# Product-key stage: the products and sums of the expert numbers on GpSimd behind its splitting of probabilities, the signed numbers one tile later on VectorE

## The reference, cut to what matters

```python
q = (x @ Wq + bq).reshape(-1, 8, 128)                 # 8 heads, two halves of 64
s1 = einsum('bhc,hnc->bhn', q[..., :64], keys[:, 0])  # 64 scores for each half
s2 = einsum('bhc,hnc->bhn', q[..., 64:], keys[:, 1])
s1t, i1 = top_k(s1, 8);  s2t, i2 = top_k(s2, 8)
all_scores = s1t[..., :, None] + s2t[..., None, :]    # 64 pairs
all_idx = i1[..., :, None] * 64 + i2[..., None, :]
scores, best = top_k(all_scores, 8)                   # 8 of the 64 pairs
indices = take_along_axis(all_idx, best)              # the expert numbers
inner = einsum('bd,bhkd->bhk', x, w_down[indices])
vals = relu(inner) * softmax(scores)
out = einsum('bhk,bhkd->bd', vals, w_up[indices])
```

## Time and profile before

| what | before |
|---|---|
| median of 3 runs | 1126.18 us (1122.7 to 1128.15) |
| the profiled execution | 1123.27 us |
| its span | 1121.3 us |
| busy in the span: PE, DVE, ACT, POOL | 86%, 73%, 45%, 36% |
| granted TensorE clock, mean of the span | 0.941 |

### The profile page before, as it was taken

The page is one execution under the profiler, slowest core; times in us unless marked ns, Lnnn a source line. Parts: engine busy times, 40 slices in busy tenths (PEclk is TensorE's granted clock), DMA queues, the critical chain, the costliest instruction groups (busy, mean ns, idle before and its releaser), DMA issues.

```text
span 1121.3 us, 21964 instructions
## 1 busy us (share of the span) xinstructions
PE 960.1 (86%) x8152; PEld 687.9 (61%) x8152; DVE 819.2 (73%) x2594; ACT 500.5 (45%) x1042; POOL 399.8 (36%) x335
## 2 busy tenths in 40 slices
PE   3587887996988888889888877899999988889997
PEld 3454444453878777778787875545545545467775
DVE  5666767568999999999999953466665565362887
ACT  1124555563344434434334332566565654344332
POOL 4664652000444453343333340455444454300000
PEclk9588999997899999999999897899999998989999
DMA  4101300000000000000000012000000000000000
GB/s 108 31 1 30 141 1 1 1 1 1 2 2 1 1 2 1 1 1 2 1 2 2 2 39 75 1 1 1 1 1 1 1 1 1 1 1 1 10 9 19
DMA packets 6720, 14.12 MB, mean 13 GB/s; under 512 B 1885, under 2 KB 4766, under 8 KB 6046
## 3 DMA queue, kind: packets, MB, share of 16 engines
q1 hardware_dynamic: 5598, 10.70, 2.9%
q0 software_dynamic: 1024, 2.10, 0.7%
HBM read 11.74 MB, written 1.05 MB: 11 GB/s over the span
## 4 chain that ended last, share of the span: by engine, by line
PE 53%; DVE 28%; issue 7%; ACT 6%; POOL 4%; DVEq 1%; POOLq 0%; DMA 0%; SPq 0%; ACTq 0%
PE quad L1859 5%; PE bank L1854 5%; PE quad L1740 4%; PE bank L1713 4%; DVE i L1134 4%; DVE w_v L1217 4%; PE bank L1765 4%; PE bank L1516 4%; PE bank L1751 4%; PE quad L1702 3%; PE bank L1629 3%; PE bank L1607 3%; PE bank L1535 2%; DVE one_u L1223 2%; ACT a_e L841 2%
## 5 line engine op out<-in xcount | busy, mean ns | idle before, releaser
L565 POOL TENSOR_TENSOR vals<-relu_in,g_sb 128x512 f32<-128x512 f32 x80 | 125.5, 1608 | 157.4 <-DVE one_u L1223 130.0
L600 POOL TENSOR_TENSOR a_e<-a_e,a_rrec 128x1024 f32<-128x1024 f32 x64 | 121.2, 1893 | 149.3 <-DVE a_rrec L1318 149.3
L1629 PE MATMUL bank<-xnT,wd 128*128 128x128 f32 x1024 | 141.1, 295 | 33.9 <-ACT relu_in L717 33.8
L1629 PEld LDWEIGHTS bank<-xnT,wd 128*128 128x128 f32 x1024 | 130.2, 205 | 45.8 <-ACT relu_in L717 41.8
L1713 PE MATMUL bank<-wu,vals 128*128 128x128 f32 x1024 | 119.5, 278 | 4.8 <-issue 4.8
L1713 PEld LDWEIGHTS bank<-wu,vals 128*128 128x128 f32 x1024 | 118.2, 195 | 4.9 <-issue 4.9
L841 ACT ACTIVATE a_e<-quad,a_negmax 128x512 f32<-128x512 f32 x128 | 86.8, 683 | 38.2 <-DVE a_negmax L1311 34.4
L1516 PE MATMUL bank<-a_kT,a_qT 32*128 32x512 f32 x344 | 83.7, 451 | 21.6 <-DVE a_q_aug L1026 13.4
L671 ACT ACTIVATE a_eT<-quad 128x512 f32<-128x512 f32 x128 | 73.9, 599 | 57.6 <-PE quad L1520 57.1
L1311 DVE TENSOR_REDUCE a_negmax<-quad 128x2 f32<-128x1024 f32 x64 | 77.9, 1217 | 22.3 <-PE quad L1740 21.6
L717 ACT ACTIVATE relu_in<-bank 128x512 f32<-128x512 f32 x128 | 73.6, 593 | 40.9 <-PE bank L1629 40.4
(11 more groups left out here) (229 smaller groups left out, 1903.3 us busy)
## 6 DMA issues: line engine op xcount, KB each, us to landing
wd<-in_pk_down SPq DMA_DIRECT2D x1, 2048.0 KB, 7.8
wu<-in_pk_up SPq DMA_DIRECT2D x1, 2048.0 KB, 12.3
wu<-in_moe_w SPq DMA_DIRECT2D x2, 1024.0 KB, 5.8
out<-h SPq DMA_DIRECT2D x4, 256.0 KB, 2.3
wd<-in_num_rows SPq DMA_DIRECT2D x1, 512.0 KB
a_eT<-in_pk_wqT SPq DMA_DIRECT2D x1, 512.0 KB, 6.4
a_eT<-in_pk_keys SPq DMA_DIRECT2D x1, 512.0 KB, 7.9
wu<-in_event_table,idx_e POOLq DMA_INDIRECT x16, 2.5
```

The costliest lines, as they stand in the source:

```text
L565: nc.gpsimd.tensor_tensor(*weigh_args(t, c, k, g_sb[:, slot, :])).then_inc(vals_pool, 1)
L600: nc.gpsimd.tensor_tensor(e1[:, g % 4], e1[:, g % 4], rrec1[:, g % 4].unsqueeze(2).to_broadcast([P, 2, S]), ALU.mult).then_inc(a1.nr, 1)
L1629: last = mm(bank[g % 2][:, q * P:(q + 1) * P], wd[:, IG * g + q, :], xnT_tile(t), start=True, stop=True)
```

## The change

The two products and six sums of the expert numbers leave VectorE and become a function of GpSimd, `pick_numbers`, that runs ahead of `split_p` of the same tile. VectorE keeps the comparisons and the softmax inverse. The two instructions for the signed numbers become a function of their own, `signed_numbers`, which VectorE runs one pass later, behind `one_hots` of the next tile. ScalarE's wait before it overwrites the candidates is set to the new count of `ij`.

```diff
+            def pick_numbers(t):
+                steps = 6 * t
+                pool.wait_ge(i8e_rdy, t + 1)
+                for s in range(2):
+                    pool.wait_ge(picked, 2 * t + s + 1)
+                    nc.gpsimd.tensor_tensor(ext[:, s], ext[:, s], i8e[:, s].rearrange("p a h k -> p a (h k)"),
+                                            ALU.mult).then_inc(ext_step, 1)
+                for s in range(2):
+                    pool.wait_ge(ext_step, steps + 1 + s)
+                    nc.gpsimd.tensor_tensor(ext[:, s, 0:4], ext[:, s, 0:4], ext[:, s, 4:8], ALU.add).then_inc(ext_step, 1)
+                for s in range(2):
+                    pool.wait_ge(ext_step, steps + 3 + s)
+                    nc.gpsimd.tensor_tensor(ext[:, s, 0:2], ext[:, s, 0:2], ext[:, s, 2:4], ALU.add).then_inc(ext_step, 1)
+                if t:
+                    pool.wait_ge(uv_rdy, t)
+                for s in (1, 0):
+                    pool.wait_ge(ext_step, steps + 5 + s)
+                    nc.gpsimd.tensor_tensor(ij[:, s], ext[:, s, 0], ext[:, s, 1], ALU.add).then_inc(ij_rdy, 1)
...
+            pick_numbers(0)
             split_p(0)
+            pick_numbers(1)
             split_p(1)
             for t in range(NT):
                 weigh_second(t)
...
                 if t + 2 < NT:
+                    pick_numbers(t + 2)
                     split_p(t + 2)
...
                 dve.wait_ge(bab_rdy, t + 1)
+                if t:
+                    dve.wait_ge(ij_rdy, 2 * t)
                 for s in range(2):
                     V.tensor_tensor(ext[:, s], bab[:, s:s + 1].to_broadcast([P, TOP, HK]), iota8[:],
-                                    ALU.is_equal).then_inc(ext_step, 1)
+                                    ALU.is_equal).then_inc(picked, 1)
...
                 V.reciprocal(pz[:, 1], pz[:, 0]).then_inc(z_rec, 1)
-                dve.wait_ge(i8e_rdy, t + 1)
-                for s in range(2):
-                    dve.wait_ge(ext_step, steps + s + 1)
-                    V.tensor_tensor(ext[:, s], ext[:, s], i8e[:, s].rearrange("p a h k -> p a (h k)"),
-                                    ALU.mult).then_inc(ext_step, 1)
                 dve.wait_ge(z_rec, t + 1)
                 V.tensor_scalar(pz[:, 2], pz[:, 1], P_UNIT, None, ALU.mult).then_inc(z_rdy, 1)
...
-                for s in (1, 0):
-                    dve.wait_ge(ext_step, steps + 7 + s)
-                    V.tensor_tensor(ij[:, s], ext[:, s, 0], ext[:, s, 1], ALU.add).then_inc(ij_rdy, 1)
+
+            def signed_numbers(t):
+                both = [P, 2, HK]
                 if t:
                     dve.wait_ge(uvpT_ps, t)
                 dve.wait_ge(ij_rdy, 2 * t + 1)
...
             half_max(1)
+            signed_numbers(0)
             half_index(1, 0, 2 * H)
...
             one_v_half(0, 1)
+            signed_numbers(1)
 
             for t in range(NT):
                 one_hots(t)
+                if t and t + 1 < NT:
+                    signed_numbers(t + 1)
                 weigh(t, 1)
```

More of the change, by code:

```diff
@@ L375, in tower @@
         m8_rdy, pair_rdy, b8_rdy, bi_rdy, bab_rdy = sem("first_max"), sem("pair_scores"), sem("pair_max"), sem("pair_index"), sem("pair_position")
-        z_sum, z_rec, ext_step, one_v_rdy = sem("z_summed"), sem("z_reciprocal"), sem("one_of_eight_steps"), sem("one_v_ready")
+        z_sum, z_rec, ext_step, one_v_rdy = sem("z_summed"), sem("z_reciprocal"), sem("number_step"), sem("one_v_ready")
+        picked = sem("positions_compared")
         uvpT_ps, uvpT_sb, onehot = sem("uvpT_in_psum"), sem("uvpT_in_sbuf"), sem("onehot_ready")
@@ L723, in expand_indices @@
                 if t:
-                    act.wait_ge(ij_rdy, t)
+                    act.wait_ge(ij_rdy, 2 * t)
                 for s in range(2):
@@ L1166, in expert_numbers @@
             def expert_numbers(t):
-                both = [P, 2, HK]
-                steps = 8 * t
                 dve.wait_ge(bab_rdy, t + 1)
+                if t:
+                    dve.wait_ge(ij_rdy, 2 * t)
                 for s in range(2):
                     V.tensor_tensor(ext[:, s], bab[:, s:s + 1].to_broadcast([P, TOP, HK]), iota8[:],
-                                    ALU.is_equal).then_inc(ext_step, 1)
+                                    ALU.is_equal).then_inc(picked, 1)
                 if t:
```

## The result

The changed kernel is slower: 1140.28 us in the median (1138.86 to 1143.33), against 1124.44 for the kernel before on the same chip, some 16 us between the medians, and a ratio of 1.0152 with a 95% interval of 1.0113 to 1.0192 (brackets behind a ratio mean this interval throughout). The prediction had started from 1126.2, the median of the three runs known then. The profiled execution took 1141.13 us (1123.27 before), its span 1139.2.

The account below looks back on a forecast made before the run. VectorE was taken to set the 25.7 us pass. Adding 4.2, less 2.1 removed and 0.52 regained, gave +1.6 a pass, 22 over 14 passes; with 2.1 ahead of the loop, +24 took 1126.2 to 1150 us, range 1130 to 1177.

Parts of the forecast that it names:

- The added 4.2 us: Per pass, GpSimd's two products and six sums, 5.1 us alone, hold up VectorE's two-input instructions for 4.2 us.
- 2.1 removed: Per pass, VectorE loses products 0.63 us, sums 1.20 and L1201's hold-up 0.27, together 2.10 us.
- the first product's 0.79: GpSimd's first product: 1.06 us less 0.12 and less about 0.15 beside VectorE's softmax inverse and scaling.
- the check on `one_v`: Earlier `one_v` collision: VectorE's loss set against GpSimd's remaining time less 0.12, as 0.06 + 1.32 against 1.43 - 0.12.
- the cancelling rival: Per pass, a collision of about 2.6 us cancels 2.1 saved and 0.5 regained: 1121 to 1131 us, chance 8%.
- L1201's 0.27: Signed-number instruction L1201, meeting `split_p`'s last instruction, takes 0.55 us against its twin's 0.28; the 0.27 would go.
- What is regained in a pass: VectorE, 2.1 us later, no longer waits for TensorE's chunk 2, so 0.52 us a pass come back.
- 1.6 by 14 passes: Net growth of 1.6 us a pass, in passes 1 to 14 (tiles 2 to 15 of `pick_numbers`): 22 us.
- the prediction's last rival: `weigh_second`'s products, late behind the chain, become the bound through ScalarE and TensorE: 1171 to 1192 us, chance 16%.
- Ahead of the loop: Tiles 0 and 1, before the loop: `w_v` starts at 273.8 us instead of 271.75, +2.1.
- that there would be no collision: GpSimd's chain would not collide with `w_v` and `one_u`: 1106 us, at most 1097, chance 12%.
- the 1.7 us: Lateness of `weigh_second` from which relu, inner products, `combine` and the next tile's chunk 0 come late too.

Follow-up runs that it names:

- the eight products that nobody waits for: Kernel before, nothing moved, with eight more GpSimd products on a buffer of their own behind `split_p`, which no engine waits for: 1166.22 us, ratio 1.0395.
- the fills: Changed kernel with the eight GpSimd instructions of `pick_numbers` as constant fills that read nothing, products and sums left out: 1105.81 us, ratio 0.9882.
- the searches: Kernel before, with GpSimd's fourth `weigh_second` product waiting for `pair_s` and two index searches ahead of the product that waits for chunk 2: 1109.52 us, ratio 0.9861.

## Why the prediction was right, and where its sizes were off

**Direction and mechanism: right.** VectorE still sets the pass, and GpSimd's instructions stand in its way. What was to show it: the second product over 4 us (5.41); `one_u` 0.4 to 0.9 longer (0.96, 0.47, 0.48 and 0.24 in the pass shown, so a little more for the first and less for the last); about 1 us of idle time before the signed numbers (0.83); the wait for chunk 2 gone (0.1 left of 6.8). The sentence that no run showed whether GpSimd sits out all 4.4 us of `w_v` has its answer: it does.

**The added 4.2 us: nearly right, one place wrong.** The piece from the first comparison to the first `weigh` grew by 14.15 - 12.22 = 1.9 us in the mean, against 2.1 predicted; with 2.1 removed, 4.0 were added. I had put the first product's 0.79 on `w_v`, which was to take 5.2. It fell on the scaling in front of it (0.94 for 0.17, so 0.77), and `w_v` keeps 4.41 but in 3 of the 16 tiles (5.39). I had counted that scaling as time in which the product runs beside VectorE. The trace before had shown otherwise, and I missed it: two scalings of four elements at the layer statistics took 1.14 us in the mean, 0.17 at the shortest elsewhere, each until a GpSimd product had ended (300 to 634 us):

```profile
L924 DVE TENSOR_SCALAR veps<-mv 128x4 f32<-128x4 f32 x2 | 2.3, 1144 | 0.2
```

The price is the same, since VectorE works in order. The part of a GpSimd instruction that costs VectorE nothing was 0.12 in my sum and is nearer 0.2 here: 1.15 - 0.96 = 0.19 for the product, 0.67 - 0.47 = 0.20 and 0.43 - 0.24 = 0.19 for the sums, whose plain durations are those of the run with the chain behind `one_u`. So a sum of 256 cost 0.47 where I had 0.61. Two side sums of the prediction are off, and its forecast adds up neither: the 0.06 has no place in the check on `one_v` (1.32 lost against 1.43 - 0.12 = 1.31), and the cancelling rival would need some four times the 0.12, not five ((5 x 0.12 + 1.6)/5 = 0.44).

**L1201's 0.27: half right.** The signed numbers now take 0.31 and 0.38 instead of 0.28 each, beside the last sum and the first instruction of `split_p`; 0.13 of the 0.27 came back. The run with the signed numbers moved alone shows it going elsewhere.

**What is regained in a pass: the mis-sized term.** I had 0.52, the wait for chunk 2. It came back, but the rest of the pass shortened by 1.02 (13.49 to 12.47). Of the other 0.5, 0.31 is `pair_s`, which went from 1.26 to 0.95 in the mean, and 0.13 the two scalings of the layer statistics, which now take 0.30 us instead of 1.14. Groups of VectorE, 300 to 634 us, before and after (the second counts 12 of the 13 tiles):

```profile
L1139 DVE TENSOR_TENSOR pair_s<-m 128x512 f32<-128x512 f32 x13 | 16.4, 1263 | 0.0
...
L1162 DVE TENSOR_TENSOR pair_s<-m 128x512 f32<-128x512 f32 x12 | 11.4, 953 | 0.0
```

`weigh_second`, delayed by the chain, meets `pair_s` with another product: the third in the pass shown (450.81 to 452.32, `pair_s` from 451.86), the fourth in the earlier trace rows. The prediction had used the collision of `pair_s` to price the new collisions, but did not ask whether the old one would stay when GpSimd's work moves. So a pass grew by 0.90 instead of 1.6, 13 x 0.7 = 9 us less in all.

**The ends of the stage: the second mis-sized term.** I multiplied 1.6 by 14 passes. But a pass in which the work is removed and the one in which most of its collision falls are neighbours. So the 15 intervals between the `w_v` are 13 with gain and cost, a first one with the gain and little of the cost, and a last one with the cost alone (+5.2). The first came to only -1.3: 2.5 us of work are gone and 1.3 us less goes to waiting for chunks and to the scaling at the statistics, but `pair_s` of that pass was held 1.3 longer, the scaling of the softmax sum 0.8 and the `one_u` 0.3. Together the two ends make +3.9 where the sum had 1.6. Timelines of VectorE for the last interval, before and after:

```profile
634.08 4.41 DVE L1217 TENSOR_TENSOR w_v<-one_v,psp 128x8192 f16<-128x8192 f16 x1
...
642.96 0.68 DVE L1232 TENSOR_TENSOR vals<-relu_in,quad 128x512 f32<-128x512 f32 x1
...
651.80 4.43 DVE L1217 TENSOR_TENSOR w_v<-one_v,psp 128x8192 f16<-128x8192 f16 x1
```

```profile
646.65 5.39 DVE L1228 TENSOR_TENSOR w_v<-one_v,psp 128x8192 f16<-128x8192 f16 x1
651.97 6.76 DVE L1234 TENSOR_TENSOR one_u<-iota_u,uv 128x2048 f16<-128x2048 f16 x4
659.57 0.31 DVE L1209 SCALAR_TENSOR_TENSOR uvp<-ij 128x128 f16<-128x128 f16 x1 [0.84 <-POOL ij L598]
...
660.10 0.68 DVE L1243 TENSOR_TENSOR vals<-relu_in,quad 128x512 f32<-128x512 f32 x1
...
666.95 2.58 DVE L1222 TENSOR_TENSOR one_v<-iota_v,uv 128x1024 f16<-128x1024 f16 x2 [4.18 <-ACT psp L768]
```

From `w_v` to the first product of `weigh` 8.88 became 13.45, +4.6, with nothing saved beside it; then 0.6 more of waiting for ScalarE's copy of `psp` (4.18 against 3.54 in the earlier trace rows), which stands behind a copy that waits 5.00 us for the late `weigh_second`, as ScalarE's timeline after shows:

```profile
664.11 0.59 ACT L779 COPY g_sb<-quad 128x512 f32<-128x512 f32 x1 [5.00 <-POOL vals L566]
```

That 0.6 is the mechanism of the prediction's last rival, in a place where VectorE has no other work.

**Ahead of the loop: right.** 273.86 where the prediction had 273.8.

So the sum, 22.4 + 2.1 = 24.5 unrounded, becomes 24.5 - 9.1 + 2.3 = 17.7, the measured 17.8, and the median of 1140.28 instead of 1150 lies within the 1130 to 1177 that was stated. The two errors have opposite signs, and that the second gave back a quarter of the first is luck. **The rivals:** that there would be no collision is refuted by the eight products that nobody waits for; what it would have given, some 20 us less, is near the 16 that the fills gave. The cancelling rival named a real weakness, that less of GpSimd's duration blocks than I had taken, but by far too much of it. The late products are the bound only when the chain stands behind `one_u` (1183.91). In the change they start 2.27 us behind the last `one_u`, more than the 1.7 us from which on the prediction had expected them to delay the next tile, and yet VectorE waits only 0.1 us for chunks in the whole stretch.

## What to carry to other kernels

Work moved from VectorE to GpSimd did not leave VectorE's path here, because it ran beside VectorE instructions with two inputs: 2.1 us of VectorE time went, and of the 5.1 us that the work takes on GpSimd 4.0 came back. So look at what VectorE does in that time, and count the GpSimd time of the moved work on VectorE's side, not its VectorE time. The gain in this kernel lay in the opposite edit, keeping GpSimd's reads away from VectorE's two-input instructions (1116.14 us, with the searches 1109.52). And where a pipeline moves work to a later pass, sum the first and the last pass apart, and ask of each old collision whether it will still be there.

## What the runs showed of the hardware

- Who yields: a GpSimd product waits out the whole VectorE instruction in whose time it is issued (5.41 us behind `w_v` for 1.15 of its own), and in turn delays the next one by 0.96 us (512 elements), 0.47 (256) or 0.24 (128). In the pass shown the two take turns, one instruction each, as long as VectorE has two-input instructions to run.
- VectorE instructions with one input can pass freely: in the trace before, the sixteen maxima of a pass take 2.11 us beside GpSimd's products (from 438.12) and 2.11 us while GpSimd is idle (from 251.25).
- But a VectorE scaling of eight elements, also with a single tensor input, was held, 0.94 us for 0.17, while in the same pass the reciprocal just ahead of it, beside the same GpSimd product, took its plain 0.20.
- Fills by GpSimd pass freely (0.55 us inside a `w_v` of 4.42). A GpSimd product with one input is held by `w_v` for all its length (4.85 us) but did not hold `w_v`, which started 0.94 us before that engine's product ended and took 4.41. The Trainium skill, SBUF — State Buffer, section "SBUF: two separate sides", has the one that starts first keep the shared port pair for the whole instruction; for these two instructions the trace differs, and the measurement decides.
- In half precision GpSimd's product of 512 elements takes 1.15 us where nothing holds it (in the run with the chain behind `one_u`), against 1.06 in single precision.
